# Layer 2 of a two-layer graph kernel: eight row pairs summed by seven block products for each two column pairs

## The reference

```
deg    = max(sum(adj != 0, -1), 1)
dinv   = rsqrt(deg)
a_norm = dinv * (adj + I) * dinv
x      = x + relu((a_norm @ h + h) @ W + b)
```

## Time and profile before

| | |
|---|---|
| median of 3 runs | 610.74 us (609.37 to 611.44) |
| the profiled execution, its own time | 611.8 us |
| its span, first to last instruction | 610.0 us |
| PE busy | 593.4 us, 97% of the span |
| DVE, ACT, POOL busy | 425.2, 362.4, 255.5 us |
| mean granted PE clock | 0.993 of full speed |

### The profile page before, as it was taken

How to read it: one execution, slowest core, us unless ns; L and a number is a source line. 1 busy time by engine, 2 the same in 40 slices (tenths; PEclk the granted TensorE clock), 3 DMA queues, 4 the chain that set the end, 5 groups by cost and what they waited for, 6 DMA issues and landing times.

```text
span 610.0 us, 13250 instructions
## 1 busy us (share of the span) xinstructions
PE 593.4 (97%) x5265; PEld 508.4 (83%) x5265; DVE 425.2 (70%) x811; ACT 362.4 (59%) x878; POOL 255.5 (42%) x361
## 2 busy tenths in 40 slices
PE   7889998999999999999999999999999999999996
PEld 5446687888888888888888888888888888888886
DVE  6897885999998999899989989988753121111111
ACT  3687667797887979797979788979642000000000
POOL 3664313554453435343525276313132374435433
PEclk8999999899999999999999999999999999999999
DMA  8908399957566565647474745010400486546401
GB/s 198 225 3 113 111 134 249 203 83 182 94 150 121 123 134 110 146 98 162 81 177 67 190 52 79 2 19 1 130 2 18 113 318 215 174 157 193 144 20 35
DMA packets 55801, 73.60 MB, mean 121 GB/s; under 512 B 20027, under 2 KB 47933, under 8 KB 54331
## 3 DMA queue, kind: packets, MB, share of 16 engines
q0 software_dynamic: 28544, 22.15, 26.5%
q1 hardware_dynamic: 24754, 46.42, 23.5%
q10 hardware_dynamic: 2441, 4.20, 2.2%
HBM read 69.31 MB, written 22.16 MB: 150 GB/s over the span
## 4 chain that ended last, share of the span: by engine, by line
PE 82%; DVE 5%; DMA 4%; issue 4%; POOL 4%; ACT 2%; ACTq 0%; POOLq 0%; DVEq 0%
PE accE L786 11%; PE accE L788 11%; PE accE L787 11%; PE accA L764 10%; PE accA L765 10%; PE accA L831 7%; PE accA L830 7%; PE accE L830 4%; PE accE L831 4%; DMA stage<-in_adj_dram 3%; POOL stage L369 1%; DVE bst L933 1%; PE pw L803 1%; PE accA L847 1%; PE pw L805 1%
## 5 line engine op out<-in xcount | busy, mean ns | idle before, releaser
L786 PE MATMUL accE<-HI,Z 128*128 128x257 f16 x676 | 185.2, 274 | 2.4 <-DVE wm L1078 2.1
L788 PE MATMUL accE<-HI,E 128*128 128x257 f16 x676 | 184.8, 273 | 0.0
L787 PE MATMUL accE<-LO,Z 128*128 128x256 f16 x676 | 184.7, 273 | 0.0
L549 ACT ACTIVATE Z<-LO,sr 128x256 f32<-128x256 f32 x338 | 151.4, 497 | 35.6 <-PE accE L788 35.6
L764 PE MATMUL accA<-HI,adjT 128*128 128x260 f16 x676 | 154.0, 273 | 0.0
L765 PE MATMUL accA<-LO,adjT 128*128 128x258 f16 x676 | 154.0, 273 | 0.0
L558 ACT ACTIVATE Z<-Z,sr 128x256 f32<-128x256 f32 x338 | 150.1, 496 | 0.2
L1034 DVE TENSOR_TENSOR Z<-adjT,Z 128x512 f32<-128x512 bf16 x169 | 127.0, 751 | 17.1 <-ACT Z L558 16.1
L1040 DVE TENSOR_TENSOR E<-Z 128x512 bf16<-128x512 f32 x169 | 129.0, 763 | 5.8
L369 POOL DMA_DIRECT2D stage<-in_adj_dram x96 | 59.3, 649 | 93.0 <-DVE adjT L1026 88.6
L831 PE MATMUL accA<-LO,adjT 128*128 128x256 f16 x416 | 91.6, 273 | 0.0
(11 more groups left out here) (127 smaller groups left out, 721.0 us busy)
## 6 DMA issues: line engine op xcount, KB each, us to landing
adjT_store<-adjT SPq DMA_DIRECT2D x11, 1664.0 KB, 6.3
stage<-in_adj_dram POOLq DMA_DIRECT2D x48, 192.0 KB, 5.0
stage<-in_adj_dram POOLq DMA_DIRECT2D x36, 224.0 KB, 5.2
adjT<-adjT_store SPq DMA_DIRECT2D x7, 896.0 KB, 6.0
adjT<-adjT_store SPq DMA_DIRECT2D x7, 768.0 KB, 6.0
stage<-adjT_store SPq DMA_DIRECT2D x4, 896.0 KB, 6.4
stage<-adjT_store SPq DMA_DIRECT2D x4, 768.0 KB, 5.8
out_dram<-late ACTq DMA_DIRECT2D x11, 256.0 KB
```

Of the source, the lines that this page charges most:

```text
L549: ins = act.activation(Z[:, n % RING, v], slw[:, m], ACT.Relu, bias=sr99[:, t:t + 1], scale=1.0 - SLOPE)
L786: pe.matmul(dst[:, 0:D + 1], zhi, HI[:, t, 0:D + 1], start=(t == 0), stop=False)
L787: pe.matmul(dst[:, 0:D], zhi, LO[:, t, 0:D], start=False, stop=False)
L788: ins = pe.matmul(dst[:, 0:D + 1], zlo, HI[:, t, 0:D + 1], start=False, stop=(t == TILES - 1))
```

## The change

For row pairs k = 4 to 11 (SEVEN) the sums over column pairs 0 to 11 are made in six groups of two column pairs (DUOS). In each group and for each v, the weights are the four 128 x 128 blocks of two column tiles and two row tiles, and the moving side is the two tiles' H cut into two halves of 128 columns. In place of the eight products of blocks (2 x 2 weights, 2 halves each) there are seven, each with its HI and LO part. Some of the seven take sums of adjacency blocks as weights (`SA`, four combinations, bf16) and some take differences of columns of H (`TH` and `TL`, f16). Column pair 12 is multiplied as before.

So: DVE makes exact f32 columns of H once (`exact_columns`), their differences (`column_sums`) and the second halves (`second_combos`), in three pieces; ACT makes the first halves (`first_combos`). For each of the eight row pairs DVE makes three of the four adjacency combinations in two parts (`adj_sums`) and POOL the fourth (`adj_difference`). After PE, ACT copies the first product out of PSUM (`first_product`), and DVE adds the products up to the sums in six instructions before it scales them (`output_seven`). `TH`, `TL` and `SA` lie in tiles of layer 1 that are no longer used, as do the exact columns. The scaling of the own term (L486) moves from POOL to ACT (`own_scaled`), and there stands behind the store of the row pair before. On DVE `second_halves1(LAST)` and `output(0)` now stand among the column sums, ahead of the last of them; on PE `dense1(LAST)` stands two column pairs later.

```diff
+    SEVEN = range(4, LAST)
+    DUOS = PAIRS // 2
+    PARTS = [(0, 3), (3, DUOS)]
+    PIECES = [(0, 2), (2, 4), (4, DUOS)]
...
+NT = 2 * DUOS * 2 * D
+TH, TL = [HI[:].rearrange("p t c -> p (t c)")[:, j * NT:(j + 1) * NT].rearrange("p (u v d) -> p u v d", v=2, d=D)
+          for j in range(2)]
+SA = LO[:].rearrange("p t c -> p (t c)").bitcast(BF16)[:, 0:2 * 4 * DUOS * 2 * P].rearrange(
+    "p (b c w i v) -> p b c w i v", b=2, c=4, w=DUOS, v=2)
+exact = [Z[:, 0:4], Z[:, 4:8], E2[:].rearrange("p n v d -> p (n v d)").bitcast(F32).rearrange(
+    "p (u v d) -> p u v d", v=2, d=D)]
+u2 = ub[:, 0, 0:P]
+p1 = ub[:, 0, P:D]
+u43 = ub[:, 1].rearrange("p (h d) -> p h d", h=2)
...
+def duo_adj(k, q, e, w0, w1):
+    return adj1[k % 3][:, 2 * w0:2 * w1].rearrange("p (w q) e i v -> p w q e (i v)", q=2)[:, :, q, e]
+def combos(k, c, w0, w1):
+    return SA[:, k % 2, c, w0:w1].rearrange("p w i v -> p w (i v)")
+def adj_sums_wait(engine, k, part):
+    engine.wait_ge(adj_ld[part][k % 3], 16 * ((k - 2) // 3 + 1))
+    if k == SEVEN[0]:
+        engine.wait_ge(unit_done, PAIRS * PAIRS)
+    if k - 2 >= SEVEN[0]:
+        engine.wait_ge(part_done[part], k - 1)
...
         if k >= 1:
             pool.wait_ge(y_ok, 2 * k)
         pool.tensor_tensor(hp, HI1[:, tiles, :], LO1[:, tiles, :], ALU.add).then_inc(hp_ok, 1)
-        pool.wait_ge(hp_ok, k + 1)
-        pool.wait_ge(selfw_ok, 1)
-        for e in range(2):
-            t = 2 * ORDER[k] + e
-            ins = pool.tensor_scalar(hpw[:, e], hp[:, e], selfw[:, t:t + 1], None, ALU.mult)
-        ins.then_inc(hpw_c, 1)
         pool.wait_ge(hpw_c, k + 1)
         pool.tensor_tensor(hpw, hpw, bass.AP(b1rep[:].tensor, 0, [[D, P], [0, 2], [1, D]]),
                            ALU.add).then_inc(hpw_ok, 1)
+    def adj_difference(k, part):
+        adj_sums_wait(pool, k, part)
+        w0, w1 = PARTS[part]
+        pool.tensor_tensor(combos(k, 2, w0, w1), duo_adj(k, 0, 0, w0, w1), duo_adj(k, 0, 1, w0, w1),
+                           ALU.subtract).then_inc(s3_ok, 1)
     for k in range(PAIRS):
+        if k + 1 in SEVEN:
+            for part in range(2):
+                adj_difference(k + 1, part)
         self_term(k)
...
+    def first_combos(j):
+        a, b = PIECES[j]
+        act.wait_ge(t34_ok, 2 * j + 2)
+        act.activation(TH[:, 2 * a:2 * b], exact[j], ACT.Copy).then_inc(th1_ok, 1)
+    def own_scaled(k):
+        act.wait_ge(hp_ok, k + 1)
+        if k == 0:
+            act.wait_ge(selfw_ok, 1)
+        for e in range(2):
+            t = 2 * ORDER[k] + e
+            ins = act.activation(hpw[:, e], hp[:, e], ACT.Copy, scale=selfw[:, t:t + 1])
+        ins.then_inc(hpw_c, 1)
...
     norm1(LAST)
     rounded1(LAST)
+    first_combos(0)
+    own_scaled(0)
     first_halves1(LAST)
+    first_combos(1)
+    own_scaled(1)
+    first_combos(2)
...
+    def first_product(k):
+        act.wait_ge(part_done[NC - 1], k + 1)
+        if k > SEVEN[0]:
+            act.wait_ge(c_ok, 4 * (k - SEVEN[0]))
+        act.activation(p1, bank([accA[1], accA[0], accE][k % 3], 0)[:, 0:P], ACT.Copy).then_inc(p1_ok, 1)
     for k in range(PAIRS):
+        if k in SEVEN:
+            first_product(k)
         store_out(k)
+        if 1 <= k < LAST:
+            own_scaled(k + 1)
...
+    def pooled_seven(k):
+        pe.wait_ge(y_ok, 2 * (k - 2))
+        first, second = bank(SETS[k % 3], 0), bank(SETS[k % 3], 1)
+        H = slice(0, P), slice(P, D)
+        pe.wait_ge(adj_ld[1][k % 3], 16 * ((k - 2) // 3 + 1))
+        for v in range(2):
+            t = 2 * LAST + v
+            for e, dst in ((0, first[:, P:P + D]), (1, second[:, 0:D])):
+                weights = adj1[k % 3][:, LAST, e, :, v]
+                pe.matmul(dst, weights, HI1[:, t, :], start=(v == 0), stop=False)
+                pe.matmul(dst, weights, LO1[:, t, :], start=False, stop=False)
+        for w in range(DUOS):
+            part = [n for n, (a, b) in enumerate(PARTS) if a <= w < b][0]
+            if w == PARTS[part][0]:
+                pe.wait_ge(s4_ok, 2 * (k - SEVEN[0]) + part + 1)
+                pe.wait_ge(s3_ok, 2 * (k - SEVEN[0]) + part + 1)
+            if k == SEVEN[0] and w in [a for a, _ in PIECES]:
+                pe.wait_ge(tl1_ok, [a for a, _ in PIECES].index(w) + 1)
+            for v in range(2):
+                a, b = 2 * w, 2 * w + 1
+                ta, tb = 2 * a + v, 2 * b + v
+                adjs = [adj1[k % 3][:, u, e, :, v] for e in range(2) for u in (a, b)]
+                sums = [SA[:, k % 2, c, w, :, v] for c in range(4)]
+                for n, (weights, hi, lo) in enumerate((
+                        (adjs[0], HI1[:, ta, H[0]], LO1[:, ta, H[0]]),
+                        (adjs[1], HI1[:, tb, H[0]], LO1[:, tb, H[0]]),
+                        (sums[3], HI1[:, tb, H[1]], LO1[:, tb, H[1]]),
+                        (sums[1], TH[:, b, v, H[1]], TL[:, b, v, H[1]]),
+                        (adjs[3], TH[:, b, v, H[0]], TL[:, b, v, H[0]]),
+                        (None, None, None),
+                        (sums[0], TH[:, a, v, H[0]], TL[:, a, v, H[0]]),
+                        (sums[2], TH[:, a, v, H[1]], TL[:, a, v, H[1]]))):
+                    if weights is None:
+                        continue
+                    dst = (first, second)[n // 4][:, n % 4 * P:(n % 4 + 1) * P]
+                    pe.matmul(dst, weights, hi, start=False, stop=False)
+                    ins = pe.matmul(dst, weights, lo, start=False,
+                                    stop=(w == DUOS - 1 and v == 1 and n % 4 == 3))
+            if w + 1 == PARTS[0][1]:
+                ins.then_inc(part_done[0], 1)
+        ins.then_inc(part_done[1], 1)
...
     for u in range(2):
         pooled(2, u)
-    for u in range(2, 5):
+    for u in range(2, 7):
         pooled(2, u)
     dense1(LAST)
-    for u in range(5, 8):
+    for u in range(7, 8):
         pooled(2, u)
     for k in range(2):
         for u in range(10, PAIRS):
             pooled(k, u)
     for u in range(8, PAIRS):
         pooled(2, u)
-    for k in range(3, LAST):
+    for k in range(3, SEVEN[0]):
         for u in range(PAIRS):
             pooled(k, u)
+    for k in SEVEN:
+        pooled_seven(k)
     for e in range(2):
         pooled_tile(LAST, e)
...
-    row_sums(LAST)
-    rounded_second1(LAST - 1)
-    second_halves1(LAST - 2)
-    row_stats1(LAST)
-    second_halves1(LAST - 1)
-    minus_mean1(LAST)
-    rounded_second1(LAST)
-    second_halves1(LAST)
...
+    def exact_columns(j):
+        a, b = PIECES[j]
+        if j == 0:
+            dve.wait_ge(unit_done, PAIRS * PAIRS)
+        dve.wait_ge(lo1_ok, 2 * b)
+        dve.tensor_tensor(exact[j].rearrange("p u v d -> p (u v) d"), HI1[:, 4 * a:4 * b, :],
+                          LO1[:, 4 * a:4 * b, :], ALU.add).then_inc(exact_ok, 1)
+    def column_sums(j):
+        q = exact[j].rearrange("p (w q) v (h d) -> p w q v h d", q=2, h=2)
+        b11, b12, b21, b22 = [q[:, :, a, :, h] for a in range(2) for h in range(2)]
+        dve.wait_ge(exact_ok, j + 1)
+        dve.tensor_tensor(b11, b12, b11, ALU.subtract).then_inc(t1_ok, 1)
+        dve.wait_ge(t1_ok, j + 1)
+        dve.tensor_tensor(b12, b22, b12, ALU.subtract).then_inc(t34_ok, 1)
+        dve.tensor_tensor(b22, b22, b11, ALU.subtract).then_inc(t2_ok, 1)
+        dve.wait_ge(t2_ok, j + 1)
+        dve.tensor_tensor(b21, b21, b22, ALU.subtract).then_inc(t34_ok, 1)
+    def second_combos(j):
+        a, b = PIECES[j]
+        dve.wait_ge(th1_ok, j + 1)
+        dve.wait_ge(t34_ok, 2 * j + 2)
+        dve.tensor_tensor(TL[:, 2 * a:2 * b], exact[j], TH[:, 2 * a:2 * b], ALU.subtract).then_inc(tl1_ok, 1)
+    def adj_sums(k, part):
+        n = 2 * (k - SEVEN[0]) + part + 1
+        adj_sums_wait(dve, k, part)
+        w0, w1 = PARTS[part]
+        dve.tensor_tensor(combos(k, 0, w0, w1), duo_adj(k, 0, 1, w0, w1), duo_adj(k, 1, 1, w0, w1),
+                          ALU.add).then_inc(s1_ok, 1)
+        dve.wait_ge(s1_ok, n)
+        dve.tensor_tensor(combos(k, 1, w0, w1), combos(k, 0, w0, w1), duo_adj(k, 0, 0, w0, w1),
+                          ALU.subtract).then_inc(s2_ok, 1)
+        dve.wait_ge(s2_ok, n)
+        dve.tensor_tensor(combos(k, 3, w0, w1), duo_adj(k, 1, 0, w0, w1), combos(k, 1, w0, w1),
+                          ALU.subtract).then_inc(s4_ok, 1)
+    def output_seven(k):
+        j = k - SEVEN[0]
+        c = [wx, wm][k % 2]
+        first, second = [bank([accA[1], accA[0], accE][k % 3], e).rearrange("p (n d) -> p n d", n=4)
+                         for e in range(2)]
+        dve.wait_ge(p1_ok, j + 1)
+        dve.wait_ge(o_ok, k - 1)
+        dve.tensor_tensor(u2, first[:, 3], p1, ALU.add).then_inc(u2_ok, 1)
+        dve.tensor_tensor(c[:, 0, 0:P], first[:, 1], p1, ALU.add).then_inc(c_ok, 1)
+        dve.wait_ge(u2_ok, j + 1)
+        dve.tensor_tensor(u43, second[:, 2:4], bass.AP(ub[:].tensor, 0, [[2 * D, P], [0, 2], [1, P]]),
+                          ALU.add).then_inc(u43_ok, 1)
+        dve.wait_ge(u43_ok, j + 1)
```

(62 more changed lines are left out.)

## The result

| | before | after |
|---|---|---|
| median, 6 runs each | 611.07 us | 613.22 us (612.48 to 614.37) |
| ratio, 95% interval | | 1.0041 (1.0026 to 1.0057) |
| span of the profiled execution | 610.0 us | 611.3 us |
| PE busy | 593.4 us | 587.4 us |
| DVE busy | 425.2 us | 526.1 us |

It lies inside the range of 602 to 617 us.

A forecast was written before the change was run, and what follows sets the result against it. PE bounds the kernel before; after the change DVE and POOL, keeping each other out, become the bound. Eight row pairs with waits sum to 89.1 against 90.9 us: 1.7 us faster, 609.0 us median, range 602 to 617.

The forecast's parts named there:

- DVE's round: DVE's work for a row pair, k = 7 to 10: 3.2 + 3.4 + 4.5 us of waits for POOL, 11.1 us.
- the wait of k = 11: PE at the last row pair: a wait of only 0.2 us, since nothing follows on DVE.
- the wait before k = 6: PE waits 2.7 us in k = 6 because its adjacency sums end late, blamed on ACT's order at k = 4.
- PE: right: PE in layer 2: 128-column matmuls take 55.9 ns, a row pair 10.28 us in place of 11.36, 8.6 us less in all.
- rival of slow matmuls: PE's 128-column matmuls are slower than taken: break-even 62 ns, far end 118 ns and 685 us; chance 0.05.
- The adjacency sums: DVE's six bf16 sums for a row pair go by 32-bit word: 0.56 us each, 3.4 us with gaps.
- The rival by element: DVE's adjacency sums go by element, 0.95 us each: a round of about 13.4 us, time 628 us; chance 0.11.
- The mechanism: A POOL operation and a DVE one with two SBUF inputs exclude each other, all but the last 0.14 us.
- the first rival: PE stays the bound because bf16 sums on DVE hardly keep POOL out, or for less: 602.7 us; chance 0.17.
- ACT's order at k = 4: On ACT the own term's scaling precedes the first product, taken 4.8 us after PE's sums, not 0.5; PE waits 2.7 us in k = 6.
- The front stage and the end: DVE's extra work before k = 4 nearly fits its idle time: PE waits 0.2 and 0.4 us; the end costs nothing.
- The late-front rival: DVE's 2048-element operations before k = 4 take 3 us, not 2.27: PE waits 4.3 us more, about 614 us; chance 0.12.

The follow-up runs named there:

- e1: The changed kernel with POOL's difference, the fourth adjacency combination, made on DVE beside the other three: 602.15 us, ratio 0.9863 to the kernel before.
- e3: The changed kernel with nobody making the differences and PE not waiting for them, so its result is not the full one: 602.75 us.
- e4: The changed kernel with POOL making each difference twice, with a wait in between: 626.46 us.
- e5: The changed kernel with the second part of each row pair's difference on DVE and the first still on POOL: 604.76 us, ratio 0.9895.
- e2: The changed kernel with ACT taking the first product of k = 4 ahead of the own term's scaling: 613.28 us, ratio 1.0041.
- e6: The kernel of e1 with the last second halves, first piece's second combinations and first output behind the last column sums on DVE: 607.0 us, ratio 0.9941.
- e7: The kernel of e1 with the own terms scaled on POOL again, not on ACT: 602.73 us, ratio 0.9878.

## Why the prediction was wrong, by its own steps

**The steps that failed** are three terms of the sum: DVE's round (11.1 us, measured 11.57), the wait of k = 11 (0.2, measured 1.3), and the wait before k = 6, whose cause was wrong too (2.7, measured 3.7). They come below, after those that held.

**PE: right.** 55.9 ns measured, as taken; a row pair of e1 takes 10.26 us against 10.28. The rival of slow matmuls is out, and with it the 81 ns of the Trainium skill ("TensorE: Matmul & The Clock Gate", Back-to-back issue gap), which this trace contradicts for a stream in which every matmul has its own load.

**The adjacency sums: right.** 0.56 us where they meet nothing, the end by 32-bit words. It agrees with the Trainium skill ("VectorE: DVE Perf Modes", The perf-mode tier table): dense bf16 sums of two tensors go at twice the f32 pace. The rival by element is out.

**The mechanism: right.** The exclusion that the rows of before showed between operations with f32 results holds for bf16 ones too, so the first rival (bf16 sums hardly keep POOL out) is out as well. e1, e3, e4 and e5 show it from both sides. That sums out of PSUM are not kept out was assumed, and the rows at k = 4 bear it out.

**DVE's round and k = 11: the terms were mis-sized.** The round was 11.57 us where the prediction had 11.1. DVE's own output part, from start to start (532.12 to 535.54), is 3.4 us in place of 3.2: y costs 0.48 for 256 elements, as the group with a column of scalars had it, where I took L1238's 0.42; the rest is small gaps. The waits are 4.8 in place of 4.5: a difference takes 1.65 us where it meets nothing, not 1.6, and 1.95 on these rows, and DVE waited 1.43 and 1.33 for the two where I had 1.26. The round of the kernel before is 11.35 us, so at 11.1 each round would still gain 0.25 and at 11.57 it loses 0.2: an error of 4% in this term decides the sign. The sum also let the rounds end with k = 10 and gave k = 11 a wait of 0.2 "since nothing follows on DVE". But the combinations for k = 11 come at the end of a full round as all the others, and PE stood still 1.3 us for them.

**ACT's order at k = 4: wrong,** by e2. The wait before k = 6 comes from the same exclusion. DVE made the sums for k = 5 ahead of the output of k = 3, under POOL's differences, so that output, ACT's queue and the y of k = 4 (2.91 us in place of 0.88) were all late. e3 and e1 keep ACT's order and have no wait there. The size was off too, 3.7 us against 2.7.

**Left out: the clock, and here it did not set the time.** The prediction let PE stand still 2.7 us and asked nothing of the clock. After 3.7 us without a matmul it was at 1.2 GHz for 3.4 us, 1.6 us of PE's time. In its place the wait at k = 7 is missing and the one at k = 8 is 0.3 shorter, together 1.6 us, since DVE, never idle here, sets when PE can go on.

**The sum again.** PE saved 8 x (11.35 - 10.26) = 8.7 us. Forecast waits were 6.8: 0.6 in front, 2.7, 3.3 and 0.2. Measured, PE stood still 9.5 us longer than before: 0.9 in front, 3.7 at k = 6, none at k = 7, and 4.9 at k = 8 to 11. With the 1.6 of clock, in place of the wait at k = 7, that is 11.1. So the rounds took 6.5 us, five times 1.3, where the forecast had 3.3 and 0.2; k = 6 took 1.0 more and the front 0.3. 11.1 - 8.7 = 2.4 us slower, and 2.4 is what the two traces show from PE's `dense1` of pair 11 to its last matmul (140.28 against 137.88 us). The span grew by less, 1.3 us, since in this execution layer 1 ended 1.1 us sooner.

**The front stage and the end: right.** DVE was busy 28 us more between 461 and 503 us (39.7 against 11.3), and that was hidden; PE stood still 0.4 us for the last halves (0.2 forecast) and 0.5 at k = 4 (0.4). The late-front rival did not come, but e6 shows how near it is.

## What to carry to other kernels

Before work is spread over DVE and POOL, add up the operations of both with two tensors in SBUF as if they ran on one engine: here a 0.56 us operation on DVE was cheaper than the same one on POOL, which took 1.65 us and kept DVE out for about 1.4 of them. The sums with an input in PSUM needn't be counted in. Where PE is the bound and two other engines must keep its pace, the slack per round is what to forecast, and the experiment to make first is to move the small operation to the engine that looks full. When PE stands still for some us, look at its clock too, and then at whether PE or another engine sets the time behind it: here it was DVE, and the slow stretch was hidden.

## What the runs showed that was not expected

- The fall of PE's clock at or just behind the end of a wait: after 3.7 us without matmuls in the changed kernel (granted 0.56 on average from 528 to 531 us), and after 3.2 in e6 (0.57 from 491 to 494). In e4 it fell at the end of a stand of 2.9 us (0.51 from 516 to 519.5) and at the end of one of 5.7 (0.57 from 534 to 537), and did not behind one of 2.0. In e5, whose longest stand is 0.9 us, and in e1 there is no fall before PE's last matmul.
- POOL's operations differ in how long they keep DVE out: about a fifth of 0.92 us for a scaling of 256 elements by a column, all but the last 0.14 us for sums of two tensors (rows of e7, and of the changed kernel), and not at all, in the rows seen, where DVE's operation has one input in PSUM.
- A difference of 768 bf16 elements takes POOL 1.65 us against DVE's 0.56, near the slope of POOL's f16 row (1.63).
